# Graph attention on 8192 nodes: adjacency fetched in quarter blocks paced by the step, values padded to 256 places, mask ring of five

## What is computed

```python
A_tilde = A + eye(n);  mask = A_tilde > 0
Wh = (H @ W.T).reshape(n, 4, 32)
e = score_l[:, :, None] + score_r.T[None, :, :]      # scores: Wh with a_l, a_r
e = where(e >= 0, e, 0.2 * e);  e = where(mask[:, None, :], e, -inf)
alpha = softmax(e, axis=2)
out = einsum('nhm,mhd->nhd', alpha, Wh)
x = layernorm(x + elu(out))
```

## Time and profile before

| | us |
|---|---|
| median of 3 runs (lowest to highest) | 1785.81 (1781.74 to 1786.43) |
| the profiled execution's own time | 1786.13 |
| its span | 1784.3 |
| PE, PEld busy | 1649.9, 1626.8 |
| DVE, ACT busy | 1685.1, 1667.3 |
| hardware DMA queue, share of 16 engines | 62.6% |

### The profile page before, as it was taken

The page is one execution under the profiler, slowest core; times in us unless marked ns, Lnnn a source line. Parts: engine busy times, 40 slices in busy tenths (PEclk is TensorE's granted clock), DMA queues, the critical chain, the costliest instruction groups (busy, mean ns, idle before and its releaser), DMA issues. The chain is left out here.

```text
span 1784.3 us, 80971 instructions
## 1 busy us (share of the span) xinstructions
PE 1649.9 (92%) x37067; PEld 1626.8 (91%) x37067; DVE 1685.1 (94%) x1905; ACT 1667.3 (93%) x1246; POOL 26.2 (1%) x36
## 2 busy tenths in 40 slices
PE   6887988899998999999999999999999999999995
PEld 6787888898998999999999999999999998999995
DVE  6999999997989989899999989999999999999997
ACT  4999999899899999999999999999999999999992
POOL 0000000000001000000000100000000100000000
PEclk9999999999999999999999999999999999999998
DMA  9995887999998786675766676666667122121111
GB/s 285 339 351 183 294 283 265 337 307 328 302 319 294 249 253 203 197 240 185 244 194 229 201 240 201 221 205 217 229 194 241 40 82 58 37 58 37 34 37 37
DMA packets 241476, 368.10 MB, mean 206 GB/s; under 512 B 12912, under 2 KB 103408, under 8 KB 239600
## 3 DMA queue, kind: packets, MB, share of 16 engines
q1 hardware_dynamic: 241136, 362.92, 62.6%
HBM read 345.57 MB, written 17.30 MB: 203 GB/s over the span
## 5 line engine op out<-in xcount | busy, mean ns | idle before, releaser
L505 ACT ACTIVATE bmask<-lrow,rtab 128x2048 fp8e4<-128x2048 f32 (+1 forms) x975 | 1548.0, 1667 | 39.4 <-PE psum L414 37.4
L414 PE MATMUL psum<-vring,cmask 128*128 128x99 bf16 x14336 | 718.0, 208 | 39.7 <-DVE cmask L730 28.5
L414 PE MATMUL psum<-vring,bmask 128*128 128x99 bf16 x14336 | 719.4, 207 | 10.8 <-DMA vring<-v_scratch 6.8
L414 PEld LDWEIGHTS psum<-vring,cmask 128*128 128x128 fp8e4 x14336 | 660.9, 98 | 52.1 <-DVE cmask L730 38.3
L414 PEld LDWEIGHTS psum<-vring,bmask 128*128 128x128 fp8e4 x14336 | 667.1, 97 | 13.8 <-DMA vring<-v_scratch 7.7
L730 DVE SCALAR_TENSOR_TENSOR cmask<-acache,bmask 128x1024 int32<-128x1024 int32 x512 | 633.1, 1237 | 25.1 <-PE psum L414 25.0
L725 DVE SCALAR_TENSOR_TENSOR bmask<-acache,bmask 128x1024 int32<-128x1024 int32 x512 | 633.8, 1238 | 6.7 <-ACT bmask L505 3.0
L706 DVE TENSOR_SCALAR bmask<-lrow,rtab 128x2048 fp8e4<-128x2048 f32 (+1 forms) x305 | 321.8, 1071 | 0.0
L383 PE MATMUL trp<-pack,abuf 128*128 128x64 bf16 x4096 | 145.6, 194 | 27.4 <-issue 14.5
L383 PEld LDWEIGHTS trp<-pack,abuf 128*128 128x128 bf16 x4096 | 133.9, 99 | 30.2 <-issue 28.6
L414 PE MATMUL psum<-vt,cmask 128*128 128x99 bf16 x2048 | 106.5, 210 | 15.1 <-DVE cmask L730 7.5
(11 more groups left out here) (64 smaller groups left out, 264.5 us busy)
## 6 DMA issues: line engine op xcount, KB each, us to landing
abuf<-in_adj_dram SPq DMA_DIRECT2D x256, 1024.0 KB, 8.2
vring<-v_scratch SPq DMA_DIRECT2D x384, 99.0 KB, 3.2
lrow<-l_scratch SPq DMA_DIRECT2D x16, 1024.0 KB, 8.2
v_scratch<-vt SPq DMA_DIRECT2D x16, 792.0 KB, 11.2
vring<-v_scratch SPq DMA_DIRECT2D x64, 198.0 KB, 7.1
cmask<-in_x_dram SPq DMA_DIRECT2D x16, 256.0 KB, 5.1
late<-in_x_dram SPq DMA_DIRECT2D x16, 256.0 KB, 5.2
out_dram<-late SPq DMA_DIRECT2D x16, 256.0 KB, 3.6
```

The lines of the kernel that those rows point to most:

```text
L414: return nc.tensor.matmul(psum[:, bank, at * S3:(at + 1) * S3], mask[:, j * P:(j + 1) * P], values, start=opening, stop=True, skip_group_c ...
L505: last = nc.scalar.activation(to, rows, ACT.Relu, bias=rtab[:, 2 * s + i, H + h:H + h + 1], scale=BIG, saturate=False)
```

## The change

- `PARTS = 4`: a block comes as four loads of 512 KB. SP's loop sends at most two of them a step before step 148, from then on one a step, or two if more than four are free to go. In passes 0 and 1 each iteration q first waits until q - 1 steps are done (`mm_done`).
- A tile's values take VW = 256 places of bf16 (before 198), the second branch beginning at place 100 (before 99), in `vt`, `v_scratch` and `vring`. GpSimd zeroes the padding once, and the first `store_v` waits for it.
- The row scores of a pass come in two loads (at s = 4 and s = 6) in place of one (at s = 3).
- The ring of B masks has BR = 5 places (before 6).

```diff
-    VW = 2 * S3
+    SP = S3 + 1
+    VW = 256
+    PARTS = 4
-    BR, CR, VR, VS, XS, AH = 6, 3, 4, 3, 6, 3
+    BR, CR, VR, VS, XS, AH = 5, 3, 4, 3, 6, 3
-        vt = sb("vt", [P, VS, 2, G, 2, S3], bf16)
+        vt = sb("vt", [P, VS, 2, G, VW], bf16)
...
-            def load_block(n, parts=range(2)):
+            def load_block(n, parts=range(PARTS)):
...
-                    rows = adj[rows_of(c, half), m * BITS * P:(m + 1) * BITS * P][part * HALF // 2:(part + 1) * HALF // 2]
-                    sp.dma_start(abuf[:, n % 2, part * SUB // 2:(part + 1) * SUB // 2],
+                    rows = adj[rows_of(c, half), m * BITS * P:(m + 1) * BITS * P][part * HALF // PARTS:(part + 1) * HALF // PARTS]
+                    sp.dma_start(abuf[:, n % 2, part * SUB // PARTS:(part + 1) * SUB // PARTS],
...
-            def load_lrow(w):
+            def load_lrow(w, u):
...
-                if w >= 2:
+                if w >= 2 and u == 0:
...
+                if n == 0:
+                    sp.wait_ge(pads_set, 1)
...
-            loaded, turned = 4, AHEAD
+            sent, turned = 4 * PARTS, AHEAD
             for q in range(Q):
                 w, s = WHERE[q]
-                while loaded < NB and loaded - 1 <= turned:
-                    load_block(loaded)
-                    loaded += 1
+                if w < JUST_MADE:
+                    wait(sp, mm_done, q - 1)
+                free = min(PARTS * (turned + 2), PARTS * NB) - sent
+                for _ in range(min(free, 2 if q < LATER_TURNS[3 * QUADS] or free > PARTS else 1)):
+                    load_block(sent // PARTS, [sent % PARTS])
+                    sent += 1
...
-                if s == 3 and w + 1 < PASSES:
+                if s in (4, 6) and w + 1 < PASSES:
                     if w == 0:
                         sp.wait_ge(l_stored, 16 * NC)
-                    load_lrow(w + 1)
+                    load_lrow(w + 1, s // 2 - 2)
...
-                pe.wait_ge(a_loaded[n % 2], 32 * (n // 2 + 1))
+                pe.wait_ge(a_loaded[n % 2], 16 * PARTS * (n // 2 + 1))
...
-                    at = i * VW + b * S3
+                    at = i * VW + b * SP
...
+            nc.gpsimd.memset(vt.rearrange("p k u t w -> p (k u t) w")[:, :, SP - 1:SP], 0.0)
+            nc.gpsimd.memset(vt.rearrange("p k u t w -> p (k u t) w")[:, :, SP + S3:VW], 0.0).then_inc(pads_set, 1)
```

More of the change, by code:

```diff
@@ L163, in gat_kernel, with parts_of @@
         zz = late[:, 4 * JC * DK:4 * JC * DK + JC * D].rearrange("p (j d) -> p j d", d=D)
+        def parts_of(n, e):
+            return vt[:, n % VS, :, :, 0:2 * SP].rearrange("p u t (b s) -> p (u t) b s", b=2)[:, :, :, e:e + E]
         VF = 2 * G * 2 * E
-        vf = vring.rearrange("p k u n -> p (k u n)").bitcast(fp32)[:, 0:VF].rearrange("p (i e) -> p i e", e=E)
-        vr = late[:, 4 * JC * DK + SUB * D:4 * JC * DK + SUB * D + VF].rearrange("p (i e) -> p i e", e=E)
+        vf = vring.rearrange("p k u n -> p (k u n)").bitcast(fp32)[:, 0:VF].rearrange("p (t b e) -> p t b e", b=2, e=E)
+        vr = late[:, 4 * JC * DK + SUB * D:4 * JC * DK + SUB * D + VF].rearrange("p (t b e) -> p t b e", b=2, e=E)
         cached = acache.rearrange("p b h m n -> p (b h m n)").bitcast(fp32)
@@ L186, in gat_kernel @@
         consts_zero, consts, w_in, a_in = sem("consts_zero"), sem("consts"), sem("w_in"), sem("a_in")
-        fac_set, ones_set = sem("fac_set"), sem("ones_set")
+        fac_set, ones_set, pads_set = sem("fac_set"), sem("ones_set"), sem("pads_set")
         w_tr, ablk_done, wa_done, wt_done = (sem(s) for s in ("w_tr", "ablk_done", "wa_done", "wt_done"))
@@ L242, in load_lrow @@
                 if narrow(w):
-                    src = l_dram[c:c + 1, h:h + 2, half * SUB:(half + 1) * SUB].rearrange("o u j n -> o u (j n)").to_broadcast([P, 2, HALF])
-                    sp.dma_start(lrow[:, w % 2], src).then_inc(lrow_in[w % 2], 16)
-                else:
-                    src = l_dram[c:c + 1, h].rearrange("o j n -> o (j n)").to_broadcast([P, CHUNK])
-                    sp.dma_start(lrow[:, w % 2].rearrange("p u n -> p (u n)"), src).then_inc(lrow_in[w % 2], 16)
+                    src = l_dram[c:c + 1, h + u, half * SUB:(half + 1) * SUB]
+                else:
+                    src = l_dram[c:c + 1, h, u * SUB:(u + 1) * SUB]
+                sp.dma_start(lrow[:, w % 2, u], src.rearrange("o j n -> o (j n)").to_broadcast([P, HALF])).then_inc(lrow_in[w % 2], 16)
             def load_v(q):
@@ L265, in store_v @@
                 sp.wait_ge(v_lo, n + 1)
+                if n == 0:
+                    sp.wait_ge(pads_set, 1)
                 sp.dma_start(v_dram[h:h + 2, :, G * g:G * g + G].rearrange("u q t w -> q u (t w)"),
-                             vt[:, n % VS].rearrange("q u t b e -> q u (t b e)")).then_inc(v_out[n % VS], 16)
+                             vt[:, n % VS].rearrange("q u t w -> q u (t w)")).then_inc(v_out[n % VS], 16)
             def as_bytes(rows, c, half, s):
@@ L288, in _ @@
                     k = (8, 10, 13).index(g)
-                    load_block(k // 2, [k % 2])
+                    load_block(k // 2, [2 * (k % 2), 2 * (k % 2) + 1])
                 if g == 11:
@@ L292, in _ @@
             sp.wait_ge(l_stored, 16)
-            load_lrow(0)
-            load_block(1, [1])
+            load_lrow(0, 0)
+            load_lrow(0, 1)
+            load_block(1, [2, 3])
             store_l(1)
@@ L332, in _ @@
                             load_xr(c, half)
-            assert loaded == NB
+            assert sent == PARTS * NB
             store_y(NC - 1, 0, ROWS_DONE[-2])
@@ L418, in values @@
                     if w < JUST_MADE:
-                        return vt[:, q // EVERY_STEPS % VS, u, 2 * (s % EVERY_STEPS) + i, b]
-                    at = i * VW + b * S3
+                        return vt[:, q // EVERY_STEPS % VS, u, 2 * (s % EVERY_STEPS) + i, b * SP:b * SP + S3]
+                    at = i * VW + b * SP
                     return vring[:, q % VR, u if narrow(w) else 0, at:at + S3]
@@ L476, in part @@
             def part(n, e, src, done):
-                nc.scalar.copy(vt[:, n % VS].rearrange("p u t b e -> p (u t b) e")[:, :, e:e + E], src).then_inc(done, 1)
+                nc.scalar.copy(parts_of(n, e), src).then_inc(done, 1)
             def highest(n):
@@ L492, in compare @@
                 if s == 0:
-                    act.wait_ge(lrow_in[w % 2], 16 * (w // 2 + 1))
+                    act.wait_ge(lrow_in[w % 2], 32 * (w // 2 + 1))
                 if q in (0, EVERY_STEPS):
@@ L639, in weigh @@
                 w4 = wh[:, G * g:G * g + G, h * E:(h + 2) * E].rearrange("p t (u e) -> p u t e", e=E)
-                v5 = vf.rearrange("p (u t b) e -> p u t b e", u=2, b=2)
+                v5 = vf.rearrange("p (u t) b e -> p u t b e", u=2)
                 for b in range(2):
@@ L646, in rest @@
             def rest(n):
-                dst = vt[:, n % VS].rearrange("p u t b e -> p (u t b) e")
                 dve.wait_ge(v_hi, n + 1)
@@ L650, in rest @@
                 wait(dve, v_lo, n)
-                nc.vector.tensor_tensor(vr, vf, dst[:, :, 0:E], ALU.subtract).then_inc(v_rest, 1)
+                nc.vector.tensor_tensor(vr, vf, parts_of(n, 0), ALU.subtract).then_inc(v_rest, 1)
             def lowest(n):
-                dst = vt[:, n % VS].rearrange("p u t b e -> p (u t b) e")
                 dve.wait_ge(v_mid, n + 1)
-                nc.vector.tensor_tensor(dst[:, :, 2 * E:S3], vr, dst[:, :, E:2 * E], ALU.subtract).then_inc(v_lo, 1)
+                nc.vector.tensor_tensor(parts_of(n, 2 * E), vr, parts_of(n, E), ALU.subtract).then_inc(v_lo, 1)
             def make_uu_exponents():
@@ L692, in compare @@
                 if s == 0:
-                    dve.wait_ge(lrow_in[w % 2], 16 * (w // 2 + 1))
+                    dve.wait_ge(lrow_in[w % 2], 32 * (w // 2 + 1))
                 n = on_vector(q)
```

## The result

The changed kernel takes 1843.03 us (median of four runs, 1837.49 to 1845.25) against 1786.12 for the kernel before: ratio 1.0312, 95% interval 1.0293 to 1.0331. Forecast were 1837 us, and slower by more than 0.3% at a chance of 0.85. The profiled execution has a span of 1841.6 us, 57.3 more than before.

The account below looks back on a forecast made before the run. The bound was taken to be PE up to step 400 or so (shared with DVE in passes 0 and 1), then DVE. The terms 47 + 4 + 7 - 4 - 10 + 6 + 1 = +51 on 1786.1 us gave 1837 us, range 1783 to 1880.

Parts of the forecast that it names:

- The late quarters: Pass 0, blocks 7 to 15: last two quarters leave one step before the turn, nine PE waits; +47 us (+29 to +54).
- The clock: Pass 0: PE's clock falls behind three of the nine waits, 2.2 us each; +7 us (0 to +20).
- Blocks 4 to 6: Pass 0: these blocks have one step and a half more and miss by less; +4 us (0 to +8).
- What is given back in pass 0: DVE gains lead over PE and the sums at the pass's end come earlier; -4 us (-8 to 0).
- Fewer gaps behind smaller loads: Passes 2 to 4: at most 1 MB of adjacency issued at once, fewer PE gaps; -10 us (between 0 and -21).
- the gaps of "issue" are late instructions: Passes 2 to 4: PE's 27.1 us in 34 gaps taken for instructions coming late behind bulk transfers.
- The ring: Passes 8 and 12: ACT's lead shrinks by up to 2.9 us and DVE waits; +6 us (0 to +15).
- Padding: Wider value loads: up to +14 us in narrow steps, down to -7 from shorter `vring` waits; net +1 us.
- B: Rival: half-size loads land within 3.6 us, PE waits 2.2 us nine times, gaps go; about 1765 us, chance 0.10.
- C: Rival: shorter ring makes DVE wait a step for ACT in each of passes 4 to 15; 1866 us, chance 0.07.
- D: Rival: no change; waits near their lower bound (+29), passes 2 to 4 lose all gaps (-21, -8); 1786 us, chance 0.05.
- E: Rival: padded table's 32 KB row pitch halves the read rate, 64 narrow steps lose 3.7 us each; 2023 us, chance 0.02.

Follow-up runs that it names:

- e1: The changed kernel with up to four quarters a step in pass 0 in place of two; 1772.77 us, ratio 0.9937 to the kernel before.
- e3: The kernel before with the paced quarters alone (ring of six, 198 places, row scores in one load); 1832.24 us, ratio 1.0268.
- e9: The changed kernel with pass 0's 1 MB store of values issued one iteration later, behind the last two quarters; 1828.38 us, ratio 1.0247 to the kernel before.
- e8: The kernel before with paced quarters, four a step in pass 0, second branch at place 100, 200 places a tile, ring of six; 1762.06 us, ratio 0.9875.
- e10: e8 without pacing: a block's four quarters issued at once, as early as the buffer allows; 1772.28 us, ratio 0.9938 to the kernel before.
- e2: The changed kernel with up to three quarters a step in pass 0 in place of two; 1776.06 us, ratio 0.9949 to the kernel before.
- e4: The changed kernel with the fetch of before, 1 MB halves as early as the buffer allows; 1793.34 us, ratio 1.0053 to the kernel before.
- e7: The kernel before with a ring of five and 256 places a tile, second branch still at place 99; 1791.71 us, ratio 1.0043.
- e6: The kernel before with the second branch at place 100 and 200 places a tile, nothing else; 1779.15 us, ratio 0.9972.
- e11: e8 with paced 1 MB halves in place of quarters, at the same rate in bytes; 1793.81 us, ratio 1.0052 to the kernel before.
- e5: The kernel before with a ring of five B masks in place of six, nothing else; 1788.47 us, ratio 1.0026.

## Why the prediction was right, point by point

**The whole.** The forecast had pass 0 at +54 us and the rest at -3. In the profiled executions pass 0 came out at +66 and the rest at -9. The step that carries the result was right; that the sum is 6 us off and not 12 is luck, because the two errors have opposite signs and different causes, as told below.

**The late quarters: right in kind, place and number.** Nine waits, from block 7 to 15, each for the reason given. e1 shows it by taking only the rate away, e3 by adding only the fetch. The waits were 52.4 us, between the rates of 49 and 62 that I bounded them by. Without a store the wait was 3.7 to 4.9 us (forecast 4.2 to 5.2), with one 7.0 to 8.3 (forecast 7.1 to 9.1); e9 shows that it is the store that makes the difference. The estimate from the Trainium skill (DMA: Bandwidth & Descriptors, "Anatomy of one DMA") had a pair down in 4.4 us; block 12's last pair, behind a store, took 165.86 - 157.47 = 8.4 us, and in e9, with the store behind it, block 10's pair left at 126.71 and PE resumed at 133.64, 6.9 us later. The trace is closer to the sum from rows (6.6) than to that fit.

**The clock: the term that was mis-sized.** I put three falls at 2.2 us, +7, in a range of 0 to +20. The stretch from step 7 to step 24 took 218.0 - 86.2 = 131.8 us. Nine cycles of 6.84 are 61.6 and the waits 52.4, which leaves 17.8 us. The price of a fall was right (17.8 / 9 = 2.0 us); the number was not: the C half behind every one of the nine waits took 2.09 to 2.86 us, so the clock fell behind all nine, that of 3.74 us included, and behind the two waits of 2.1 us before blocks 5 and 6. It does not fall behind every such wait: e9 has one of 3.89 us without. PE's busy time in pass 0 rose from 111.15 to 132.73 us for the same matmuls. With it the stretch is 61.8 us longer, where I had +47 and +7.

**Blocks 4 to 6:** forecast +4, measured 42.3 - 37.3 = +5.0 us for steps 0 to 6, with two waits, 4.2 us in sum.

**What is given back in pass 0:** forecast -4. Steps 25 to 31 and the start of pass 1 gave 0.7 us. PE's waits there did not get shorter: 1.33 us for a C mask and 4.85 for the taking of the sums before, 1.56 and 4.89 after. The term was wrong, if small.

**Fewer gaps behind smaller loads: wrong for the changed kernel.** I gave -10 us to passes 2 to 4 and named it as a sign. They came out 0.6 us shorter in sum, with 21.3 us of gaps of "issue" (13.9 + 7.4) in place of 23.1 (11.7 + 11.4). PE's waits in passes 2 to 4, before (305.4 to 645.3 us) and in e3 (364.1 to 698.0 us):

```profile
PE psum L414 <- issue: 11.7, 16, 1.5
PE trp L383 <- issue: 11.4, 11, 1.5
```

```profile
PE psum L418 <- issue: 9.4, 14, 1.5
PE trp L387 <- issue: 5.4, 8, 0.9
```

With the fetch alone the gaps are 14.8 us and the three passes 6.1 us shorter, so the mechanism is there, at a little over half the size. The kernels with quarters and 198 or 200 places have 14.8 to 17.0 us of gaps in these passes (e3, e8, e10), those with quarters and 256 places 19.0 to 21.3 (the changed kernel, e1, e2, e9), those with halves issued at once 17.4 to 28.0 (before, e4 to e7). That points to the wider loads of values giving back what the smaller loads of adjacency gain; with one trace each and that much scatter it is not shown.

What made up for it lies where I had forecast nothing: passes 5 to 11 are 10.3 us shorter in sum. The offset alone has 8.7 us there (e6), the fetch alone 8.8 (e3), where PE's waits for `vring` and gaps of "issue", 6.8 us before, are 1.1: in pass 8, for one, PE had waited 2.6 us for `vring` behind a block and the residual rows. The two gains don't add up in the changed kernel. e10 and e8 show that size and pacing each have a part.

**That the gaps of "issue" are late instructions** I had only taken for likely. The traces bear it out: each of the gaps of PE between 300 and 1650 us (30 in the kernel before, 36 in the changed one, 24 in e8, 57 in e11) ends 1.15 to 1.65 us after a 16 KB packet of the instruction queue ends, where a moment picked at random does so in 9% of cases. These packets take about 1.0 us whether a gap follows or not, so they come late and not slowly; what holds them up was not tested.

**The ring:** forecast +6 within 0 to +15. e5: +0.26%, 4.6 us (1.4 to 7.9), in the passes named, 8 and 12; pass 9 took no longer, and in pass 13 DVE didn't wait for ACT at all. The way it reaches PE was another: ACT's copy of a turned block comes late, not the mask (e5).

**Padding:** +1 for the wider loads, and nothing for the offset. The offset was wrong: it gives 0.28%, 5 us (e6), since a step without a turn is 0.04 us shorter on PE. The wider table costs some 6 us by the estimate under e7, where I had +1. That the two together come out near +1 is luck as well.

**The rivals.** B (1765, short landings) fell: in pass 0 no last pair let PE go within 5.1 us of its issue (1.4 and the shortest wait, 3.7). C (the ring decides) fell with e5, which has 4.6 us and not 35. D (no change) fell: the waits were 52.4 us and not 38, and passes 2 to 4 kept their gaps. E (the row pitch of 32 KB): e7 has that pitch, and its values land in 3.3 us at the median in wide steps and 7.6 in narrow ones, where 99 and 198 KB took 3.2 and 7.1.

## What to carry to other kernels

When loads are paced by a consumer's progress, write down for each load the event that releases it and the event that wants it, and compare the distance with the landing time, behind whatever else was issued in between. A rate that matches demand on average (two quarters a step, four in two steps) has no slack if it starts with none. And price the clock with each gap on PE: here nine waits of 5.8 us on average cost 7.8 each. When a ring is made shorter, look at all that its writer does in order: here ACT's copies came late before its masks did.

## What I had not expected of the hardware

**The byte offset of the moving values sets PE's pace.** With 99 bf16 columns against 128 fp8 weight columns a half step of 32 matmuls takes 1.44 us for B masks (tiles at bytes 0 and 396), 1.43 for C masks (198 and 594, or 198 and 710), and 1.41 at bytes 0 and 400, 0 and 512, 200 and 600, all of them multiples of 8. Whether 8 is the step that counts was not tested. Over the kernel it is 0.28%.

**Spreading 1 MB loads was worse than bunching them.** In e11 one load in two steps brought 32 gaps of "issue", 25.6 us, between 600 and 1400 us, where e8 with half the size each step had 0.2, and the kernel before, with 2 MB at once every four steps, had 2.2 us of them from 1000 to 1400 us. All of e11's gaps end just behind an instruction packet, as told above; that load and packet fall together every second step would explain their number, but I did not test it.

In both pairs (e10 against e6, e8 against e11) 512 KB beat 1 MB. The Trainium skill (DMA: Bandwidth & Descriptors, "Rules for kernel authors") advises at least 1 MiB a transfer for bandwidth. That is another aim than here, and no run measures the bandwidth of either size; the pairs compare the time of the whole kernel.
